# Moving the ranking of the source nodes from layer 0 of a graph network into layer 1's hold and scatter pass

## The reference, cut to what matters

```python
# layer 0
aggr_out = segment_sum(x[src] * edge_weight[:, None], dst, N)
# layer 1: h = x @ W_lin + b_lin, ee = edge_attr @ W_edge + b_edge
x_i, x_j = h[src], h[dst] + ee
alpha = (x_i * att_i).sum(-1) + (x_j * att_j).sum(-1)
alpha = where(alpha >= 0, alpha, 0.2 * alpha)
e = exp(alpha - segment_max(alpha, src, N)[src])
alpha = e / (segment_sum(e, src, N)[src] + 1e-16)
out = segment_sum(x_j * alpha[:, :, None], src, N).mean(heads) + bias
```

## Time and profile before

| | us |
|---|---|
| device time, median of 3 runs | 11548.99 (11494.93 to 11647.08) |
| profiled execution, span | 11537.7 |
| layer 0: first to last gather (L822) | 40.1 to 2625.1 |
| layer 0: ranking half of the block | about 1194 to 2674 |
| layer 1: node tables, on DVE from | 2774.7 |
| layer 1: first to last scatter (L1303) | 2943.0 to 5018.1 |

### The profile page before, as it was taken

How to read it: one execution, slowest core, us unless ns; L and a number is a source line. 1 busy time by engine, 2 the same in 40 slices (tenths; PEclk the granted TensorE clock), 3 DMA queues, 4 the chain that set the end, 5 groups by cost and what they waited for, 6 DMA issues and landing times. The chain is left out here.

```text
span 11537.7 us, 92744 instructions
## 1 busy us (share of the span) xinstructions
PE 3146.5 (27%) x19432; PEld 2586.9 (22%) x19432; DVE 6821.8 (59%) x9436; ACT 4714.2 (41%) x6523; POOL 6567.8 (57%) x6626
## 2 busy tenths in 40 slices
PE   1111588882000000000023555555554200000002
PEld 1111477772000000000013444444443100000001
DVE  6777666664222311159962777777775566666664
ACT  1111466661211111137731666666662343334342
POOL 5656666665677777730023666666662466666663
PEclk9999767675555555555555677776775655555555
DMA  3332322222333323235522444444441666666662
GB/s 91 88 83 78 80 60 71 71 82 26 121 112 111 107 94 106 103 125 207 205 104 52 117 118 124 117 116 122 118 117 39 194 202 201 199 202 205 203 201 70
DMA packets 722783, 1395.92 MB, mean 121 GB/s; under 512 B 409552, under 2 KB 439453, under 8 KB 715095
## 3 DMA queue, kind: packets, MB, share of 16 engines
q0 software_dynamic: 287072, 587.19, 19.4%
q1 hardware_dynamic: 406786, 639.32, 17.0%
q10 hardware_dynamic: 28852, 168.65, 4.0%
HBM read 827.48 MB, written 602.51 MB: 124 GB/s over the span
## 5 line engine op out<-in xcount | busy, mean ns | idle before, releaser
L822 POOL DMA_INDIRECT l_rows<-in_x,l_idx x1568 | 1613.7, 1029 | 1010.1 <-issue 431.0
L2445 POOL DMA_INDIRECT l_rows<-table,l_idx x1568 | 1487.5, 949 | 1032.2 <-issue 483.2
L1925 POOL DMA_INDIRECT l_rows<-h,l_idx x1568 | 1540.3, 982 | 882.1 <-issue 442.4
L1303 POOL DMA_INDIRECT rows<-l_rows,l_idx x1568 | 1548.9, 988 | 554.0 <-issue 526.3
L1960 PE MATMUL l_made<-l_kv_w,l_rows_t 128*128 128x256 f32 x3136 | 1117.3, 514 | 1041.1 <-ACT l_kv L1990 402.5
L1960 PEld LDWEIGHTS l_made<-l_kv_w,l_rows_t 128*128 128x128 f32 x3136 | 761.2, 259 | 1279.5 <-issue 1147.1
L2521 ACT ACTIVATE l_lifted<-l_rows,l_up 128x256 f32<-128x256 f32 x1568 | 653.2, 463 | 824.0 <-DVE l_half_low L2473 527.1
L1698 PE MATMUL l_wide<-l_diag,l_ones 128*128 128x384 f32 x4 | 3.3, 926 | 3218.0 <-DVEq L1728 3218.0
L1259 ACT COPY l_rows<-l_run 128x1792 f32<-128x1792 f32 x56 | 191.6, 3421 | 1636.1 <-POOLq L88 1359.5
L1292 DVE TENSOR_TENSOR l_rows<-l_run,l_weights_ps 128x56 f32<-128x56 f32 x56 | 12.0, 215 | 1371.0 <-POOLq L88 1168.7
L1698 PEld LDWEIGHTS l_wide<-l_diag,l_ones 128*128 128x128 f32 x4 | 1.0, 312 | 3218.9 <-DVEq L1728 3218.9
(11 more groups left out here) (393 smaller groups left out, 12672.9 us busy)
## 6 DMA issues: line engine op xcount, KB each, us to landing
sums<-l1s_out ACTq DMA_DIRECT2D x56, 1988.0 KB, 7.1
sums<-l_out SPq DMA_DIRECT2D x112, 924.0 KB
spread<-zeros SPq DMA_DIRECT2D x28, 3612.0 KB
l_spread<-spread SPq DMA_DIRECT2D x112, 903.0 KB
l1s_rows<-rows SPq DMA_DIRECT2D x56, 1008.0 KB, 4.7
spread<-zeros SPq DMA_DIRECT2D x56, 938.0 KB
l_spread<-spread SPq DMA_DIRECT2D x56, 938.0 KB
sums<-l_out ACTq DMA_DIRECT2D x56, 896.0 KB
```

The source lines that it names most:

```text
L822: pool.indirect_dma_start(rows[:, b, t], None, a["x"], bass.IndirectOffsetOnAxis(ap=idx[:, b, t:t + 1], axis=0)) \
L1303: pool.indirect_dma_start(g["rows1_d"], bass.IndirectOffsetOnAxis(ap=idx[:, b, t:t + 1], axis=0), rows[:, b, t], None).then_inc(sent[b], 16)
L1925: pool.indirect_dma_start(rows[:, c.r, t, 0:C], None, g["h2_d"], bass.IndirectOffsetOnAxis(ap=idx[:, c.r, t:t + 1], axis=0)).then_inc(got[ ...
L2445: pool.indirect_dma_start(rows[:, b, t], None, g["table3_d"], bass.IndirectOffsetOnAxis(ap=idx[:, b, t:t + 1], axis=0)) \
```

## The change

The histograms of both keys stay in layer 0, but each is spread over one half of the chunks: `dst` over chunks 0 to 27, `src` over chunks 28 to 55, with 8 histogram steps in a chunk. They are a class of their own now. All of layer 0 weighs on DVE into PSUM, and nothing paces the gathers. The ranking, its position output and its wait leave layer 0. The split keys are kept in SBUF for layer 1.

Layer 1's table block runs the first turn of 8 ranking steps beside its scatters. The hold and scatter pass runs the other 27 turns, 4 steps in each of chunks 0 to 53. The positions stay in SBUF and are copied into `idx` by DVE, so that SP no longer loads them. PSUM is now full with the ranking, so `data`, `dot` and the edge weights move to SBUF, and `tensor_copy` into `data` reads and writes SBUF. The ranking's float tiles lie in the buffers that the next pass uses (`held.run`), and `ends.row` and `prod` of the table block in `held.scale`. Between ordering and layer 0 there is one more barrier with a clearing of semaphores.

```diff
+        ordering(nc, a, sem, dict(locals()))
+        clear_semaphores()
...
 # layer0, POOL
-                        for t in range(T):
-                            if counting and t % PACE == 0:
-                                hist_paced(h, b, t // PACE)
-                            if turn is not None and t % PACE == 0:
-                                ranking.paced(pool, turn, t // PACE)
+                        for t in range(T):
                             pool.indirect_dma_start(rows[:, b, t], None, a["x"], ...)
...
 # layer0, DVE
+                    def both(n, h):
+                        for b in range(2):
+                            hist.vector(v, n, h * 2 + b)
+                            weigh(h + HALF * n, b)
+                            sum_rows(h + HALF * n, b)
...
-                    ranking.vector_start(v, g["first"]["src"])
-                    with v.Fori(0, turns // 2) as h:
-                        for b in range(2):
-                            for r in range(TURN):
-                                ranking.vector_step(v, h * 2 + b, r)
-                            wait(v, weighed[b], h + 1)
-                            sum_rows(h + turns // 2, b, data[:, b])
-                    ranking.vector_end(v)
...
 # layer1, table block: PE, ACT and DVE each run turn 0
+                    ranking.vector_start(v, g["first"]["src"])
+                    for r in range(TURN):
+                        ranking.vector_step(v, 0, r)
...
 # layer1, hold and scatter pass
-            data = s.ps("l1_data", [P, W, T + 1])
+            data = s.sb("l1_data", [P, W, T + 1])
+            dot = s.sb("l1_dot", [P, T, H])
...
+                @block.tensor
+                def _(pe):
+                    with pe.Fori(1, LAST + 1) as turn:
+                        for r in range(TURN):
+                            ranking.tensor_step(nc, pe, turn, r)
...
 # ACT, for h in 0..LAST-1 and each b (keeps is L1255, fill is L1259 and L1260)
+                            ranking.scalar_step(nc, act, h + 1, b * STEPS)
+                            keeps(h, b)
+                            ranking.scalar_step(nc, act, h + 1, b * STEPS + 1)
+                            fill(h, b)
+                            ranking.scalar_step(nc, act, h + 1, b * STEPS + 2)
+                            ranking.scalar_step(nc, act, h + 1, b * STEPS + 3)
...
 # DVE: hold is L1280 to L1288, score is L1292 and the copy of the positions
+                    def score(h, b):
+                        wait(v, free[b], h + 1)
+                        v.drain()
+                        v.tensor_tensor(rows[:, b, :, F1:R1], run[:, b, C:W, 1:].rearrange("p f t -> p t f"), dot[:], ALU.add)
+                        v.tensor_copy(idx[:, b], ranking.pos_f[:, bass.ds((h * 2 + b) * T + SB, T)]).then_inc(scored[b], 1)
...
+                                ranking.vector_step(v, h + 1, b * STEPS)
+                                hold(h, b)
+                                ranking.vector_step(v, h + 1, b * STEPS + 1)
+                                score(h, b)
+                                ranking.vector_step(v, h + 1, b * STEPS + 2)
+                                ranking.vector_step(v, h + 1, b * STEPS + 3)
+                    ranking.vector_end(v)
+                    for b in range(2):
+                        hold(LAST, b)
+                        score(LAST, b)
```

More of the change, by code:

```diff
@@ L837, in _ @@
                     for n in range(len(KEYS)):
-                        ranking.hist_tensor_start(nc, pe, n)
+                        hist.tensor_start(nc, pe, n)
                         with pe.Fori(0, turns) as h:
-                            ranking.hist_tensor(nc, pe, n, h)
-                        counts.tensor(nc, pe, g, ranking.hist(n), n + 1)
-                    ranking.tensor_start(nc, pe)
-                    with pe.Fori(0, turns) as h:
-                        for r in range(TURN):
-                            ranking.tensor_step(nc, pe, h, r)
+                            hist.tensor(nc, pe, n, h)
+                        counts.tensor(nc, pe, g, hist.sums[n], n + 1)
                 @block.vector
@@ L1148, in _ @@
                     nc.scalar.copy(rows[:, :, 0:C], x[:]).then_inc(copied, 1)
+                    ranking.scalar_start(nc, act)
+                    for r in range(TURN):
+                        ranking.scalar_step(nc, act, 0, r)
+                @block.tensor
+                def _(pe):
+                    ranking.tensor_start(nc, pe)
+                    for r in range(TURN):
+                        ranking.tensor_step(nc, pe, 0, r)
                 @block.vector
@@ new lines, in fill @@
+                    def fill(h, b):
+                        wait(act, scanned[b], h + 2)
+                        wait(act, free[b], h + 1)
+                        nc.scalar.copy(rows[:, b, :, 0:C].rearrange("p t f -> p f t"), run[:, b, 0:C, 1:])
+                        nc.scalar.copy(rows[:, b, :, C:C + D5], attr[:, b]).then_inc(filled[b], 1)
+                    with act.Fori(0, LAST) as h:
+                        for b in range(2):
+                            ranking.scalar_step(nc, act, h + 1, b * STEPS)
[4 more added lines that the diff above has]
+                            ranking.scalar_step(nc, act, h + 1, b * STEPS + 3)
```

331 lines of the change are left out of this document (150 added, 181 removed).

## The result

The changed kernel took 12356.81 us (median of 4, 12316.3 to 12440.2), beside 11544.1 for the kernel before: a ratio of 1.073, 95% interval 1.068 to 1.078. The forecast was 11268, and its range ended at 11500. The profiled execution has a span of 12371.1, 833.4 us above that of before.

What follows compares the result with a forecast made beforehand. It took POOL's indirect DMAs as layer 1's bound, and layer 0's gathers as held back by other work. Layer 0 -639, small edits +9, collisions +349 gave -281: a span of 11257, a time of 11268 us, range 11050 to 11500.

Steps and rivals of the forecast that it cites:

- Part 1: Layer 0: without pacing and ranking, POOL's gathers set the pace at 1.265 us each; last gather at 2023, -639 us.
- Part 3: Layer 1's pass: the added ranking steps fit beside POOL's scatters, so POOL stays the bound at 35.4 us a chunk.
- the ring: Layer 1's pass: DVE, PE and ACT waiting for each other in a circle, with POOL waiting for the score at its end.
- the chain becomes the bound: Rival, layer 1's pass: waits among DVE, PE and ACT set the pace, 58 us a chunk, 12139 us; chance 0.07.
- Part 4: Layer 1's pass: DVE operations with two SBUF inputs hold up POOL's scatters, +349 us, bounds 0 and 659.
- whole length: Rival, layer 1's pass: each collision costs POOL the DVE operation's full duration, 659 instead of 349, 11578 us; chance 0.16.
- Part 2: Small edits: extra barrier and clearing 5 us, table block's 8 ranking steps 4, dropped position loads 0; +9 us.

## Why the prediction was wrong, point by point

**Part 1, "so POOL is the bound": the step that failed first.** It set DVE's 17.5 us of work against POOL's 35 and took for granted that the two run side by side. The work was right (19 us a chunk with one gather in 28). That both proceed at once was not: in the first pair and on A, B and D DVE keeps its rate for some 12 us of the stream and then falls to a step every 5 to 20 us until POOL waits. -602 us at the last gather became -99. Where nothing stands still the step is exact: the last gather ended at 2019 on chip C (loops of layer 0 written out), and 2023 was the forecast.

The rows of before already had it. In the first half DVE had 825 us of work in 1154, and 16 steps of 1.42 with 6 us for weighing and scan are 29 of the 41 us of a chunk. The missing 12 I gave to the pacing's waits without asking what POOL waited for. L251's 293 us of idle time, 251.8 of it "remote", were DVE's, not POOL's.

**Part 3, "the pass stays POOL's", the step that cost most.** That the ring by itself is shorter than POOL's 35.4 was right: 27 us a chunk with one scatter in 28, and 28 us of waiting for L1278 in the whole pass on chip C. That its engines keep their pace beside POOL's stream was not. Beside POOL's stream on the other chips it took 2965/56 = 53 us a chunk. The rival "the chain becomes the bound" thus named the right wait and a size near the right one, 58, past its point of 46.7, but not the cause. A ring that nothing overlaps in was not what happened; its engines were stopped. That this rival's time, 12139, lies near the 12357 measured is luck: it had +1220 for the pass where +891 came, and the full gain of layer 0, which did not come. Slower than before had a chance of 0.06 in all.

**Part 4, the collisions, +349.** The mechanism was right, and its size depends on the chip. In the trace after, the scatters' mean is 1009 ns, (1009 - 958) x 1568 = 80 us over the median's: DVE mostly stands while POOL works. On chip C the mean is 1199, 378 us over the median's, 8% above the forecast. With two pauses on chip D it is 1193, so what the pauses give back the collisions take in part. The copy L1263 took 1.87 us at the median of its line (56 of them, 104.4 us), where I took 1.1, and 2.08 with PSUM; its double rate did not show. On chip C the rival "whole length" (659) is out as well. The range's upper end was summed wrong by 21 us: gathers at 1.32 and collisions of 8 us a chunk give 10919 + 92 + 448 = 11459, not 11480, which changes nothing here.

**Part 2, +9.** The new barrier showed no cost: the first gather starts at 35.5 instead of 40.1. The term that went wrong is the table block's 8 ranking steps, for which 4 us stood. From the last of that block's scatters to the first of the pass (starts) there were 28.7 us before and 53.0 after, on chip D 28.5 and 55.0: the steps had not kept pace beside the block's 98 scatters. On chip C it is 29.0.

**The sum on a chip without standstills.** It would have missed there too, and that is the second failed step: the sum was made against a layer 0 that held standstills of its own. The kernel before takes 10390 on C and E. Layers 2 and 3 and the rest behind the last scatter are the same code in both, 10436.2 - 4681.7 = 5754.5 us on C, so its last scatter starts at about 4636. With chip D's 2013.5 us of scatters and 318.4 between, an estimate from two chips, its last gather comes at about 2304, and not at 2620. By this estimate the change can save some 290 us there and not 600, and the collisions took 378. The estimate is made from chip C's time before, so it can't be checked by it. What was measured is 10438 and 10441 against 10393, one execution each, both with straight code in layer 0. Neither the change alone nor a trace of the kernel before was taken on such a chip.

**What stays open.** Whether the two kinds are of chips or of sessions, what the one has that the other has not, and what stops the engines. The runs exclude the number of DVE's and PE's instructions, the bytes, the loops of DVE, PE and ACT in layer 0 and, as far as the packets recorded tell, the fetching of code. Left are the number of indirect DMAs and their rows and semaphore updates (the kernel counts 16 for each gather), and POOL being busy as such. Updates without gathers were not tried, and fills without gathers only where there are no standstills. No version that computes the same beat the kernel before. The nearest are the straight code on C (0.4%, one execution), both stages paced on A (0.6%) and two pauses in a chunk on D (0.7%, but 4.9% on C).

## What to carry to other kernels

A wait that seems to cost an engine time may be what lets the others run: before unpacing a stream of indirect DMAs, take out the pacing alone and time it. Idle time put down to "remote" or "issue", on an engine whose instructions have nothing to wait for, is the sign to look for, and it was there before the change. And before a stage's time is read as a bound, see whether the same kernel takes the same time on another chip.

## What the runs showed of the hardware

- One kernel, unchanged, took 10387 to 10393 us on two chips and 11518 to 11797 on three (11544 in the first pair), each in one session. 766 us of the 1147 between the first trace and chip C lie behind layer 1's pass (6520.5 against 5754.5 us for the same code); the idle time of POOL's two lines in layers 2 and 3 differs by 687.
- In a standstill single instructions of PE come 0.7 us apart (3446.01, 3446.73; 3448.12, 3448.82), and SP's DMA instructions of L802 last 0.70 us at the median instead of 0.35 on chip C. In the two places shown it ends 4 and 9 us after the end of POOL's last indirect DMA.
- A standstill does not begin with the stream: DVE's histogram steps keep 1.42 us for some 12 us beside gathers 1.25 us apart, then come 5 to 20 us apart.
- A fill and a drain of POOL, which add 2.4 us, before every fourth gather remove all standstills of layer 0 (1431 to 29 us), before every fourteenth most of them (281 us left).
- A drain of POOL behind indirect DMAs cost 2.4 us after 7 of 256 bytes a row, and 6.3 after 14 in layer 3 (chip E against C).
- DVE operations with two SBUF inputs delay POOL's indirect DMAs: 378 us over their median in 1568 scatters beside 4 ranking steps and one scan a chunk (chip C), the longest 4.78 us.
